# Self-attention with generated weights: where and when the softmax denominators are inverted

## The reference

```python
h = _layernorm(hs, ln1_g, ln1_b)
qkv = _student_linear(h, *ca)
q, k, v = jnp.split(qkv, 3, axis=-1)
q, k, v = (split(q), split(k), split(v))          # 16 heads of 16
scores = jnp.einsum('bhqd,bhkd->bhqk', q, k) / float(HD) ** 0.5
scores = jnp.where(causal, scores, jnp.asarray(-10000.0, scores.dtype))
attn = jax.nn.softmax(scores, axis=-1)
o = jnp.einsum('bhqk,bhkd->bhqd', attn, v)
o = _student_linear(o, *cp)
hs = hs + o
```

## Time and profile before

| | us |
|---|---|
| median of 3 runs | 3768.4 (3765.77 to 3771.09) |
| profiled execution | 3750.74 |
| its span | 3748.9 |
| the stage's turns 1 to 14 and the rest, from 2934.7 to 3110.8 of the span | 176.0 |

### The profile page before, as it was taken

One profiled execution on the slowest core, in us unless ns is written; L12 is line 12 of the kernel. 1 busy time (PEld: TensorE's weight loads), 2 busy tenths in 40 slices (PEclk: granted clock), 3 DMA queues, 4 the chain that ended last, 5 costly groups with the idle time before them and its releaser, 6 DMA issues. The chain is left out here.

```text
span 3748.9 us, 76885 instructions
## 1 busy us (share of the span) xinstructions
PE 3184.8 (85%) x30862; PEld 2176.7 (58%) x30862; DVE 1819.2 (49%) x4553; ACT 1188.1 (32%) x2326; POOL 913.9 (24%) x751
## 2 busy tenths in 40 slices
PE   7886999999996875879857899879997788999988
PEld 2333445544566773555624555569996675566655
DVE  7886443344124342442267666643334582355543
ACT  1222222222213322131232655522221452244432
POOL 1000432233000000230624877712111220104000
PEclk9887999999997986998978999979998888999989
DMA  4212000000116011341731111058886210021100
GB/s 147 68 56 75 21 9 8 16 8 0 49 31 43 4 23 30 82 129 45 228 87 33 32 29 28 10 213 331 329 326 234 95 55 15 28 73 54 43 8 15
DMA packets 183358, 291.65 MB, mean 78 GB/s; under 512 B 85585, under 2 KB 153639, under 8 KB 173716
## 3 DMA queue, kind: packets, MB, share of 16 engines
q1 hardware_dynamic: 175572, 266.95, 23.3%
q0 software_dynamic: 7488, 20.46, 1.7%
HBM read 243.33 MB, written 28.48 MB: 73 GB/s over the span
## 5 line engine op out<-in xcount | busy, mean ns | idle before, releaser
L2581 PE MATMUL ps<-L_ffn_xsT,arena 128*128 128x128 f32 x2584 | 305.9, 277 | 0.8 <-DVE L_ffn_xsT L2397 0.7
L2581 PEld LDWEIGHTS ps<-L_ffn_xsT,arena 128*128 128x128 f32 x2584 | 298.5, 194 | 2.9 <-DVE L_ffn_xsT L2397 2.7
L161 POOL TENSOR_TENSOR rstd<-nsc,mhalf 112x4 f32<-112x4 f32 (+1 forms) x24 | 40.1, 1669 | 954.6 <-DVE nsc L154 953.6
L793 POOL TENSOR_TENSOR L_xattn_rn<-L_xattn_ss,mhalf 125x16 f32<-125x16 f32 (+1 forms) x64 | 185.7, 2901 | 324.4 <-DVE L_xattn_ss L847 324.4
L3242 POOL TENSOR_TENSOR L_xattn_pT<-L_xattn_pT,L_xattn_keep 125x678 int32<-125x678 int32 x128 | 190.4, 1509 | 71.9 <-ACT L_xattn_pT L3497 71.9
L686 PE MATMUL ps<-L_attn_prod,arena 128*32 128x448 f32 (+31 forms) x672 | 157.2, 537 | 44.5 <-DVE L_attn_prod L508 44.5
L2489 ACT ACTIVATE L_ffn_silu<-ps,arena 128x128 f32<-128x128 f32 x280 | 102.9, 368 | 269.3 <-PE ps L2581 252.5
L2406 DVE SCALAR_TENSOR_TENSOR L_ffn_hT<-ps,arena,L_ffn_silu 128x128 f32<-128x128 f32 x280 | 97.9, 350 | 156.8 <-ACT L_ffn_silu L2489 156.8
L961 PE MATMUL ps<-arena,L_xattn_cT 128*125 128x512 f32 x384 | 170.3, 596 | 4.3 <-DVE L_xattn_unit L840 4.3
L508 DVE TENSOR_TENSOR L_attn_prod<-arena,L_attn_k 128x448 f32<-128x448 f32 (+10 forms) x336 | 160.4, 545 | 2.3 <-PE ps L686 2.3
L976 PE MATMUL ps<-L_xattn_unit,L_xattn_cn 125*128 125x512 f32 x336 | 159.2, 634 | 0.0
(11 more groups left out here) (574 smaller groups left out, 6713.2 us busy)
## 6 DMA issues: line engine op xcount, KB each, us to landing
arena<-in_L_ffn_up SPq DMA_DIRECT2D x35, 2056.0 KB, 7.7
arena<-in_L_ffn_down SPq DMA_DIRECT2D x35, 1152.0 KB, 8.8
L_xattn_ctxT<-in_ctxT SPq DMA_DIRECT2D x48, 375.0 KB, 3.8
arena<-in_L_ffn_up SPq DMA_DIRECT2D x43, 384.0 KB, 4.5
L_attn_a<-L_attn_skew SPq DMA_DIRECT2D x16, 784.0 KB, 5.8
L_xattn_ctx<-in_ctx SPq DMA_DIRECT2D x30, 375.0 KB
arena<-L_xattn_kp SPq DMA_DIRECT2D x64, 93.8 KB, 3.3
L_xattn_mask<-in_mask SPq DMA_DIRECT2D x32, 164.1 KB, 8.5
```

Of the source, the lines that this page charges most:

```text
L793: nc.gpsimd.tensor_tensor(rn[0:r, i], ss[0:r, i], core.mhalf[0:r, 0:H], ALU.pow).then_inc(po_r.step("root", i), 1)
L2581: ins = nc.tensor.matmul(ps[:, 2 + b % 4, half * TS:(half + 1) * TS], self.up(i % WU, k, half * HM + m), xsT[:, i % 2, k], start=(k == 0), ...
```

## The change

- `den` becomes 128 rows of 14 and has three buffers instead of two, as has `op`. The DMA of the denominators in `results` writes the same numbers in this form. `results(n)` waits for `divided(n-3)` instead of `divided(n-2)`.
- `inverses` takes the reciprocal of `den` into `turned_over`, 128 rows of 14. A new DMA on SP (`inverses` there) brings this to `inverse`, 16 rows of 112, with semaphores `i_in`. SP issues it for i-2 after `results(i-1)` and ahead of `placed(i+3)`.
- DVE takes the reciprocal of i-2 at the head of turn i instead of that of i-1 after the second half of the subtraction. `update` is of i-3, `divided` of i-2.
- PE spreads i-2 after the keys and ahead of `attend(i)`, instead of i-1 at the turn's end, and waits for `i_in` there. It writes bank 3 instead of bank 7. The scores wait for `divided(i-3)` as well, the second half of the transposes waits for no division. The output product is of i-3, and the queries come ahead of the wait for the second half of the copied scores.
- The end of each loop is written anew for one more sequence in flight.

```diff
-        o, op, on = sb("o", [128, 2, NQ * T]), sb("op", [128, 2, KD * T]), sb("on", [128, 2, KD * T])
-        den, inverse, row = sb("den", [H, 2, T]), sb("inverse", [H, 2, T]), sb("row", [T, D])
+        o, op, on = sb("o", [128, 2, NQ * T]), sb("op", [128, 3, KD * T]), sb("on", [128, 2, KD * T])
+        den, inverse, row = sb("den", [128, 3, H * T // 128]), sb("inverse", [H, 2, T]), sb("row", [T, D])
+        turned_over = sb("turned_over", [128, 2, H * T // 128])
...
-        Q_, K_ = (1, 0), (2, 3)
+        Q_, K_, SPREAD = (1, 0), (2, 3), 3
...
             def results(n):
                 sp.wait_ge(ac_p.sem, ac_p.at(n, "o"))
+                if n >= 3:
+                    sp.wait_ge(ve_d.sem, ve_d.at(n - 3, "divided"))
+                by_tile = lambda t: t.rearrange("p (j t) -> p j t", t=T)
+                sp.dma_start(den[:, n % 3], by_tile(o[0:128:Z, n % 2])).then_inc(o_in[n % 3], DMA)
...
+            def inverses(n):
+                sp.wait_ge(ve_r.sem, ve_r.at(n, "inverse"))
                 if n >= 2:
-                    sp.wait_ge(ve_d.sem, ve_d.at(n - 2, "divided"))
-                by_tile = lambda t: t.rearrange("p (j t) -> p j t", t=T)
-                sp.dma_start(den[:, n % 2], by_tile(o[0:128:Z, n % 2])).then_inc(o_in[n % 2], DMA)
...
+                    sp.wait_ge(pe_w.sem, pe_w.at(n - 2, "spread"))
+                sp.dma_start(inverse[:, n % 2], turned_over[:, n % 2]).then_inc(i_in[n % 2], DMA)
...
                 if i >= 1:
                     results(i - 1)
+                if i >= 2:
+                    inverses(i - 2)
                 if i + 3 < NB:
                     placed(i + 3)
...
             for i in range(NB):
+                if i >= 2:
+                    inverses(i - 2)
                 if i + 1 < NB:
                     shifted(i + 1, 0)
-                if i >= 2:
-                    update(i - 2, 0)
+                if i >= 3:
+                    update(i - 3, 0)
                 if i + 1 < NB:
                     shifted(i + 1, 1)
-                if i >= 1:
-                    inverses(i - 1)
                 if i + 3 < NB:
                     queries(i + 3)
...
                 prepared(i)
-                if i >= 1:
-                    divided(i - 1)
+                if i >= 2:
+                    divided(i - 2)
...
                     if i >= 3:
-                        ten.wait_ge(ve_o.sem, ve_o.at(i - 3, "out"))
+                        ten.wait_ge(ve_d.sem, ve_d.at(i - 3, "divided"))
+                    if i >= 4:
+                        ten.wait_ge(ve_o.sem, ve_o.at(i - 4, "out"))
                     scores(i + 1)
...
                     ten.wait_ge(ac_x.sem, ac_x.at(i + 3, "xT"))
-                if i >= 2:
-                    ten.wait_ge(ve_d.sem, ve_d.at(i - 2, "divided"))
                 turned(i, 1)
...
+                    project(i - 3, 0)
+                if i + 3 < NB:
+                    queries(i + 3)
                 if i + 1 < NB:
                     ten.wait_ge(ac_s.sem, ac_s.at(i + 1, "scores", 1))
+                else:
+                    ten.wait_ge(ve_d.sem, ve_d.at(i - 3, "divided"))
                 if i + 3 < NB:
-                    queries(i + 3)
                     keys(i + 3)
+                if i >= 2:
+                    spread(i - 2)
                 attend(i)
                 if i + 2 < NB:
                     values(i + 2)
                 if i + 4 < NB:
                     turn(i + 4, 6)
-                if i >= 1:
-                    spread(i - 1)
```

More of the change, by code:

```diff
@@ L4345, in build @@
         norm, twice, zeroed, bias, late = (core.semaphore(n) for n in ("norm", "twice", "zeroed", "bias", "late"))
-        qk_in, o_in = ([core.semaphore(f"{t}_in{i}") for i in range(2)] for t in ("qk", "o"))
+        qk_in, i_in = ([core.semaphore(f"{t}_in{i}") for i in range(2)] for t in ("qk", "inverse"))
+        o_in = [core.semaphore(f"o_in{i}") for i in range(3)]
         following = run.following
@@ L4379, in results @@
                 sp.wait_ge(ac_p.sem, ac_p.at(n, "o"))
-                if n >= 2:
-                    sp.wait_ge(ve_d.sem, ve_d.at(n - 2, "divided"))
-                by_tile = lambda t: t.rearrange("p (j t) -> p j t", t=T)
-                sp.dma_start(den[:, n % 2], by_tile(o[0:128:Z, n % 2])).then_inc(o_in[n % 2], DMA)
-                for g in range(HQ):
-                    sp.dma_start(op[g % 2 * 64:(g % 2 + 1) * 64, n % 2, g // 2 * T:(g // 2 + 1) * T],
-                                 by_tile(o[g * Z + 1:g * Z + 1 + HD, n % 2])).then_inc(o_in[n % 2], DMA)
+                if n >= 3:
+                    sp.wait_ge(ve_d.sem, ve_d.at(n - 3, "divided"))
+                by_tile = lambda t: t.rearrange("p (j t) -> p j t", t=T)
+                sp.dma_start(den[:, n % 3], by_tile(o[0:128:Z, n % 2])).then_inc(o_in[n % 3], DMA)
+                for g in range(HQ):
+                    sp.dma_start(op[g % 2 * 64:(g % 2 + 1) * 64, n % 3, g // 2 * T:(g // 2 + 1) * T],
+                                 by_tile(o[g * Z + 1:g * Z + 1 + HD, n % 2])).then_inc(o_in[n % 3], DMA)
+            def inverses(n):
+                sp.wait_ge(ve_r.sem, ve_r.at(n, "inverse"))
+                if n >= 2:
+                    sp.wait_ge(pe_w.sem, pe_w.at(n - 2, "spread"))
+                sp.dma_start(inverse[:, n % 2], turned_over[:, n % 2]).then_inc(i_in[n % 2], DMA)
             sem, arena = run.ahead
@@ L4403, in _ @@
             results(NB - 1)
+            inverses(NB - 2)
+            inverses(NB - 1)
         @block.gpsimd
@@ L4464, in inverses @@
             def inverses(n):
-                dve.wait_ge(o_in[n % 2], (n // 2 + 1) * (HQ + 1) * DMA)
+                dve.wait_ge(o_in[n % 3], (n // 3 + 1) * (HQ + 1) * DMA)
                 if n >= 2:
-                    dve.wait_ge(pe_w.sem, pe_w.at(n - 2, "spread"))
-                nc.vector.reciprocal(inverse[:, n % 2], den[:, n % 2]).then_inc(ve_r.step("inverse"), 1)
+                    dve.wait_ge(i_in[n % 2], n // 2 * DMA)
+                nc.vector.reciprocal(turned_over[:, n % 2], den[:, n % 3]).then_inc(ve_r.step("inverse"), 1)
             def divided(n):
@@ L4473, in divided @@
                     dve.wait_ge(pe_o.sem, pe_o.at(n - 2, "out"))
-                nc.vector.tensor_tensor(on[:, n % 2], op[:, n % 2], ps[:, 7, 0:KD * T], ALU.mult).then_inc(ve_d.step("divided"), 1)
+                nc.vector.tensor_tensor(on[:, n % 2], op[:, n % 3], ps[:, SPREAD, 0:KD * T], ALU.mult).then_inc(ve_d.step("divided"), 1)
             def update(n, bank):
@@ L4545, in _ @@
                 prepared(i)
-                if i >= 1:
-                    divided(i - 1)
-            update(NB - 2, 0)
+                if i >= 2:
+                    divided(i - 2)
+            inverses(NB - 2)
             inverses(NB - 1)
+            update(NB - 3, 0)
+            divided(NB - 2)
             divided(NB - 1)
-            update(NB - 1, 1)
+            update(NB - 2, 1)
+            update(NB - 1, 0)
         @block.scalar
@@ L4593, in results @@
                 if n >= 2:
-                    act.wait_ge(o_in[n % 2], n // 2 * (HQ + 1) * DMA)
+                    act.wait_ge(o_in[(n - 2) % 3], ((n - 2) // 3 + 1) * (HQ + 1) * DMA)
                 act.wait_ge(pe_p.sem, pe_p.at(n, "pv"))
@@ L4667, in spread @@
             def spread(n):
-                ten.wait_ge(ve_r.sem, ve_r.at(n, "inverse"))
+                ten.wait_ge(i_in[n % 2], (n // 2 + 1) * DMA)
                 for m in range(KD):
-                    ins = nc.tensor.matmul(ps[:, 7, m * T:(m + 1) * T], self.of_head[:, m * 128:(m + 1) * 128], inverse[:, n % 2], start=True, stop=True)
+                    ins = nc.tensor.matmul(ps[:, SPREAD, m * T:(m + 1) * T], self.of_head[:, m * 128:(m + 1) * 128], inverse[:, n % 2], start=True, stop=True)
                 ins.then_inc(pe_w.step("spread"), 1)
@@ L4730, in _ @@
                     ten.wait_ge(ac_s.sem, ac_s.at(i + 1, "scores", 0))
-                if i >= 2:
+                if i >= 3:
                     if i + 1 == NB:
-                        ten.wait_ge(ve_o.sem, ve_o.at(i - 3, "out"))
-                    project(i - 2, 0)
+                        ten.wait_ge(ve_o.sem, ve_o.at(i - 4, "out"))
+                    project(i - 3, 0)
+                if i + 3 < NB:
+                    queries(i + 3)
                 if i + 1 < NB:
                     ten.wait_ge(ac_s.sem, ac_s.at(i + 1, "scores", 1))
+                else:
+                    ten.wait_ge(ve_d.sem, ve_d.at(i - 3, "divided"))
                 if i + 3 < NB:
-                    queries(i + 3)
                     keys(i + 3)
+                if i >= 2:
+                    spread(i - 2)
                 attend(i)
@@ L4744, in _ @@
                     turn(i + 4, 6)
-                if i >= 1:
-                    spread(i - 1)
+            ten.wait_ge(ve_d.sem, ve_d.at(NB - 3, "divided"))
+            ten.wait_ge(ve_o.sem, ve_o.at(NB - 4, "out"))
+            project(NB - 3, 0)
```

(8 more changed lines are left out.)

## The result

The change makes the kernel slower. On the chip of its first timing the median is 3795.7 us (3787.2 to 3801.9) against 3770.3 (3765.8 to 3773.8), a ratio of 1.0067 with a 95% interval of 1.0052 to 1.0082. On a second chip it is 3790.0 against 3772.8, ratio 1.0049 (1.0032 to 1.0067). The forecast was +13 us; these are +25.4 and +17.3.

What follows compares the result with a forecast made beforehand. The vector loop through DVE and the queue loop through SP were taken to set the changed kernel's turns. Terms -4.9 + 11.8 + 2.6 + 3.9 = +13.4 us took the median of 3768.4 to 3781 us, range 3764 to 3794.

Steps and rivals of the forecast that it cites:

- turns 1 to 3: Stage start: queries no longer held up by the reciprocal in turn 1, so turn 3 starts earlier; 4.9 us gained.
- Reciprocal: DVE: 14 columns instead of 112 take an estimated 0.24 us, at the turn's head where DVE is idle; 0.77 us leave the chain.
- Vector loop: Chain from scores through DVE's turn to the division, which the next scores wait for: 9.5 us plus the weight step.
- Queue loop: Chain from attend through keys, SP's issues of placed and results, the inverses' landing and spreading: 10.8 to 10.9 us a turn.
- Turns 3 to 14: Queue loop or vector loop sets each turn, whichever is longer: 136.6 us against 124.8 before, 11.8 us lost.
- Tail: End of the stage: attend(15) some 0.8 us later and the second DMA's landing added; 2.6 us lost.
- Clock: PE: six half-clock turns, as before, lengthen the loops; 3.9 us lost.
- the clock stays low in all turns: Rival: PE's longer gaps make all turns start at 1.2 GHz; +20 us, 3788 us; chance 0.16.
- The inverses land late: Rival: the inverses' DMA lands later than 2.4 us; 3.0 us gives 3788, 3.6 gives 3795; chance 0.12.
- Only the vector loop binds: Rival: the queue runs ahead, turns 3 to 14 take 130.1 us, the whole +3 us, 3771; chance 0.22.
- Faster: Rival: the gap at the weight loads closes, turn 2 lasts 12 us not 21.7, the whole is 3761; chance 0.08.

Runs made afterwards that it cites:

- e1_direct: Changed kernel with the reshaping of den and the second DMA undone, reciprocal kept at the head of DVE's turn: stage 175.5 us, ratio to before 1.0002.
- the second trace: Changed kernel profiled again without any edit, on the chip of the follow-up runs: stage 191.8 us, ratio to before 1.0049.
- e5_direct_divide: Changed kernel with reshaping and second DMA undone and divided(i-2) moved right after the queries on DVE: stage 157.3 us, ratio to before 0.9927.
- e2_first: Changed kernel with SP issuing the inverses' DMA ahead of results instead of behind: stage 190.6 us, ratio to before 1.0045.
- e3_divide: Changed kernel with divided(i-2) moved on DVE ahead of front, kept and the weight step: stage 192.5 us, ratio to before 1.0045.
- e4_both: Changed kernel with the edits of e2_first and e3_divide together: stage 173.3 us, ratio to before 0.9998.
- e9_after_spread: Changed kernel with its six 1 MB weight loads issued two, two, one, one over turns 0 to 3, not three and three: stage 193.9 us, ratio to before 1.0052.
- e7_act_queue: e4_both with the inverses' DMA issued by ACT after its copies of the scores, not by SP: stage 162.6 us, ratio to before 0.9957.

## Why the prediction was off in size, step by step

The direction and both loops were right. The size was +13 us where +25 and +17 were measured, and the first median lay 1.7 us above the range's end. The step that failed is the term for the turns 1 to 3: a gain of 4.9 us was forecast, and 0.7 was measured.

*Reciprocal.* Estimated 0.24 us, measured 0.232. That it lies where DVE is idle and costs nothing is shown from the other side by e1_direct, where 0.83 us cost nothing.

*Vector loop.* 9.5 us plus the weight step. Turns 5, 6 and 7 were to take 11.1, 11.8 and 11.8; they took 11.3, 12.0 and 12.7, and 11.3, 12.0 and 12.2 in the second trace. Right, and shown by e5_direct_divide.

*Queue loop.* 10.8 to 10.9 us forecast; 11.04 measured, from a shorter landing (1.85, not 2.4) and more time in the nine issues (6.38, not 5.8). That the two errors cancel is luck; the loop itself is shown by e2_first with e3_divide and e4_both. (The prediction counts 528 pieces in turn 5, the trace of before has 660 packets there; nothing in the sum hung on it.)

*Turns 1 to 3: the step that failed.* The forecast was a gain of 4.9 us. The trace has 0.7: turn 3 starts 34.2 us after turn 1, not 30.0, and before it was 34.9. The second trace has 34.3. The 4.2 us of the miss are these: SP reached the inverses 2.8 us later than I had it, since the burst's issues took 9.8 us and I had taken the 7.2 of before; the DMA then took 2.5 us and not 3.5; and PE, idle for 16.3 us, worked at half clock, so that the spreading took 1.1 us and not 0.5, and attend and the values up to the next scores 4.0, not 2.2. I had neither the longer hold in the burst nor the half clock in this term.

I also had results(0) landing when it did before. It landed 19.1 us after the start of turn 1 instead of 16.5. e1_direct, with the old layout of the denominators, shows the same 19.1, so the layout is not the cause; the second burst now starts 7 us earlier, and so do four DMAs of queries and keys, and which of them delays it is not shown. This did not add to the 4.2 us: SP reached the inverses only 7.5 us after the reciprocal had started.

*Turns 3 to 14.* Forecast 11.8 us lost and 3.9 for the clock. Up to the start of the transposes of turn 15 (3139.32) these took 143.3 us instead of 124.8, so 18.5 lost, 2.8 more than forecast. Turn 10 had 15.9 us instead of 12.4. In the second trace turn 10 had 12.5, and the same stretch took 137.0 us (2989.19 to 3126.16), 12.2 lost, 3.5 less than forecast.

*Tail.* Forecast 2.6 lost, measured 3.1, in the second trace 4.2.

*Clock.* The rival that the clock stays low in all turns is out: the turns 5 and 6 of both traces ran at 1.00. A part of the turns did run at a mean of 0.7 to 0.9, about as many as before. The Trainium skill's warning of idle gaps (TensorE: Matmul & The Clock Gate, "Why this matters for your kernels") held for the long wait of turn 2, where the trace shows 0.69 over the turn. In the others the traces agree with it only in part: in the second trace of the change the single pause of 3.46 us ahead of turn 7 was followed by a turn at 0.86 and the pause of 2.02 us ahead of turn 6 by one at 1.00, but turn 6 of the earlier trace rows ran at 0.69 after a pause of 1.35 us.

*Sum.* 4.2 + 2.8 + 0.5 are the 7.5 us between the forecast stage (+13.4) and the first trace (+21.0). The second trace has +15.8, and there the three are 4.3, -3.5 and 1.6: only the term of the turns 1 to 3 missed by the same in both traces. Between the stage's +21.0 and the first median's +25.4 lie 4.4 us; the interval of that ratio reaches from 19.6 to 30.9 us, so whether anything outside the stage belongs to the change stays open. Nothing in the second comparison asks for it.

*The rival cases.* "The inverses land late" is out by their landing (median 1.8 us). "Only the vector loop binds" is out by e3_divide and e4_both. "Faster" is out; what it needed, a second burst that does not hold SP up, was tried with e9_after_spread, and the loads were then in the way a turn later.

## What to carry to other kernels

When a wait is moved off one engine's path by a second DMA, follow that DMA into its queue: what is issued ahead of it, and whether any of that waits for what the DMA releases. A buffer or bank that is freed by an instruction at the end of an engine's turn puts all of that turn on the path, so an instruction that frees something goes ahead of the work that nobody waits for. Two loops of nearly one length hide each other: open each alone and little moves, open both and the whole gain appears.

## What the runs showed of the hardware

- The reciprocal on DVE took 833 ns for 16 x 112, 252 for 112 x 16 and 232 for 128 x 14 (partitions x columns): about 6.1 ns for each column more. The number of partitions leaves no mark that these three could show.
- A DMA of 7 KB from one place of the on-chip memory to another landed in 1.8 us from its issue, in 128 pieces of 56 bytes on one side; one of 56 KB takes 2.3. In most turns the small pieces were not the price, the place in the queue was. Beside the loads of 1 MB the same DMA took up to 4.7 us, and in e7_act_queue 5.7.
- The queue that issues loads was held up in its issues. One issue of the second burst took 3.29 us here, 4.02 in e1_direct and 3.25 in the kernel before; most other issues of loads took 0.4 to 0.6. The whole burst took 9.8 us where it began 8 us after the first (here and in e1_direct), and 7.2 where it began 16 us after it (before).
- Results(0) landed 2.6 us later in the change and in e1_direct, where the next queries and keys and the second burst are issued 7 us earlier. This makes it likely, and does not show, that DMAs issued behind a DMA delay its landing.
